# Quantised FFN at the end of a two-layer kernel: GpSimd scales the second half of the hidden blocks, and VectorE's and ScalarE's order changes

## The chip, the cores and the metric

The kernel runs on one core of a Trainium2 chip. Five engines work side by side, each through its own queue in order: TensorE (PE; its weight loads are shown as PEld), VectorE (DVE), ScalarE (ACT), GpSimd (POOL), and SyncE (SP), which here issues transfers. They meet through semaphores. The metric is the device time of one execution in microseconds; shown is a median of three runs. The profile is of one other execution.

## The reference, cut to what matters

Two layers on x of 16 x 256 tokens by 256 features. Only the last step, the quantised FFN of layer 1, is touched:

```python
def fake_quant_nvfp4(x, global_scale):          # blocks of 16 elements
    amax = jnp.max(jnp.abs(xb), axis=-1, keepdims=True)
    sc8 = clip(amax / 6 * global_scale, 0, 448).astype(float8_e4m3fn)
    dq = sc8 / global_scale
    a = jnp.clip(jnp.abs(xb) / safe_dq, 0.0, 6)
    q = jnp.sign(xb) * _FP4_VALS[jnp.digitize(a, _FP4_MIDS)]
    return (q * dq).reshape(sh)

gate_out = nvfp4_linear(x, gate_w, s_in)        # 256 -> 1024, x and w both quantised
up_out = nvfp4_linear(x, up_w, s_in)
hidden = silu(gate_out) * up_out
out = x + nvfp4_linear(hidden, down_w, s_in_down)   # 1024 -> 256, hidden quantised
```

## The kernel before

The 4096 tokens are 32 tiles of 128. The stage takes them in eight groups of four tiles. Each group is quantised as two pairs: `hh[0]` holds the hidden values of tiles 0 and 1 (128 partitions x 2048 f32), `hh[1]` those of tiles 2 and 3. There is no planner: every engine's program is written out by hand, six of the eight groups run in a loop, and semaphores count what is done.

VectorE's `group(g)` is a software pipeline. It quantises the hidden values of group g while it makes those of group g+1 (tiles t to t+3, with t = 4g + 4):

- `hidden_sizes` and `rows_sizes` (line 1837 and 1839): maxima over blocks of 16, from absolute values that ScalarE wrote (`s_ah`, `s_ax`).
- `block_scales` (1843 to 1849): the e4m3 scales and, in `inv4`, their reciprocals.
- `rows_scaled` (1871): the next rows x4 times their reciprocals. ScalarE then writes them as f16 (`rows_half`, 773), VectorE clamps (1877), rounds (1880) and multiplies by the scale (1886, `xq`).
- `hidden_scaled(p)` (1874): pair p of `hh` times the reciprocals of its blocks, into `wraw[:, p]`. ScalarE writes the f16 `hf[p]` from it (`hidden_half`, 972), VectorE clamps (1877), rounds (1880) and multiplies by the scale (`hidden_quantised`, 2169, `hq[p]`).
- `product(t, u)` (2177): silu times up, in two halves of 512 columns, from a bank and from `sil`, into `hh[u // 2]`.
- `results(g-1)` (2184): the down product of the group before, from banks 1 and 7, plus the residual X2, into `yo`, in two steps k = 0 and 1.

ScalarE's `group(i)` runs in this order: `rows_half`, the copies of turned hidden values for the down product (`hidden_out`, 985), `hidden_half(i, 0)`, the copy of the turned rows (`x_out`, 954), `hidden_half(i, 1)`, then `silu` (962) of four tiles in turn with `hidden_size` (absolute values, 967), and the norm of later rows (765, 769).

TensorE's loop turns quantised rows (1432) and hidden values (1462), multiplies down (1473), and then `ahead` runs gate (1441) and up (1450) of the four tiles; a gate product waits for the silu of the tile before, an up product for the product on VectorE. GpSimd does nothing in this stage, and SyncE sends `yo` out.

Of the kernel before, what the change touches and what calls it, by code (L numbers as in the profile page):

```python
# [7 lines left out]
ALU = mybir.AluOpType  # L8
# [9 lines left out]
P = 128  # L18
EPS = 1e-5
FAR = 1.0e6  # L20
FP4_MAX, FP8_MAX, BLOCK = 6.0, 448.0, 16
# [39 lines left out]
def two_layers_kernel(nc, x, itok, ctxT, ctxO, mask, w_redT, wgT, W1, b1, W2, b2,  # L61
# [8 lines left out]
    NTILE = NT // P  # L70
# [34 lines left out]
    with es:  # L105
# [3 lines left out]
        def sem(name):  # L109
            return es.enter_context(nc.semaphore(name))  # L110
# [71 lines left out]
        inv = sb("inv", [P, NIX], F32, ea)  # L182
# [88 lines left out]
        hh = [sb(f"hh{h}", [P, NQ], F32, ec) for h in range(2)]  # L271
# [8 lines left out]
        wraw = sb("wraw", [P, 3, FT * D], F32, ec)  # L280
# [38 lines left out]
        NBX, NBH = 4 * D // BLOCK, 2 * NQ // BLOCK  # L319
# [4 lines left out]
        inv4, scb = carve(5120, 320, F32), carve(5440, 160, BF16)  # L324
# [3 lines left out]
        def top(a):  # L328
# [23 lines left out]
        s_idle = sem("s_idle")  # L352
# [5 lines left out]
        s_S, s_sub, s_exp, s_pT, s_pTe, s_pv, s_cn, s_cT, s_cTe, s_wo, s_fin = [  # L358
            sem(n) for n in ("s_S", "s_sub", "s_exp", "s_pT", "s_pTe", "s_pv", "s_cn", "s_cT", "s_cTe", "s_wo", "s_fin")]
# [4 lines left out]
        n_cb, n_xn, n_ct, n_xt, n_kv, n_kb, n_q, n_qe = [sem(n) for n in ("n_cb", "n_xn", "n_ct", "n_xt", "n_kv", "n_kb", "n_q", "n_qe")]  # L364
        n_kc, n_va, n_bo = s_cke, s_cve, s_wo
        n_S, n_add, n_fo, n_sub, n_exp, n_pT, n_pTe, n_pv = [sem(n) for n in ("n_S", "n_add", "n_fo", "n_sub", "n_exp", "n_pT", "n_pTe", "n_pv")]
        n_cn, n_cT, n_cTe, n_wo, n_fin = [sem(n) for n in ("n_cn", "n_cT", "n_cTe", "n_wo", "n_fin")]
        s_wl, s_wmx, s_war, s_wq, s_wT, s_wTe = [sem(n) for n in ("s_wl", "s_wmx", "s_war", "s_wq", "s_wT", "s_wTe")]
        s_dst, s_dsd, s_xq, s_xqT, s_xqe, s_gm, s_um, s_sil, s_hq, s_hT, s_hTe, s_dn, s_y = [
            sem(n) for n in ("s_dst", "s_dsd", "s_xq", "s_xqT", "s_xqe", "s_gm", "s_um", "s_sil", "s_hq", "s_hT", "s_hTe",  # L370
                             "s_dn", "s_y")]
        s_h, s_gs, s_nm2, s_x4 = sem("s_h"), sem("s_gs"), sem("s_nm2"), sem("s_x4")
        s_ax, s_ah, s_vx, s_vh, s_fx, s_fh = [sem(n) for n in ("s_ax", "s_ah", "s_vx", "s_vh", "s_fx", "s_fh")]
        s_out = sem2("s_out")
# [90 lines left out]
        def _(pool):  # L465
# [166 lines left out]
            with pool.Else():  # L632
# [7 lines left out]
                for k in range(1, SLOTS):  # L640
                    weight_scaled(k)


        @block.scalar
        def _(act):
# [310 lines left out]
            def silu(t, u, first=False):  # L956

                for k in range(2):
                    act.wait_ge(s_gm, 2 * t + (k + 1))
                    if not first:  # L960
                        act.wait_ge(s_h, 2 * t + (k - 3))
                    act.activation(sil[:, u % 2, k * 512:(k + 1) * 512], bank[2 + k][:], ACT.Silu,  # L962
                                   scale=gmx[:, 8:9]).then_inc(s_sil, 1)

            def hidden_size(t, u):
                act.wait_ge(s_h, 2 * t + 2)
                act.activation(absh[:, u * FF:(u + 1) * FF], top(hh[u // 2][:, (u % 2) * FF:(u % 2 + 1) * FF]),
                               ACT.Abs).then_inc(s_ah, 1)

            def hidden_half(g, p):  # L970
                act.wait_ge(s_vh, g * 2 + (p + 1))
                act.mul(hf[p][:], top(wraw[:, p, :]), ABOVE).then_inc(s_fh, 1)

            x_out(0)
# [12 lines left out]
            def group(i, first=False, last=False):  # L987
                t = i * 4 + 4
                rows_half(i + 1)
                if not first:  # L990
                    hidden_out(i - 1, 2)
                hidden_half(i, 0)
                if not first:
                    hidden_out(i - 1, 3)
                x_out(i + 1)
                hidden_half(i, 1)
                silu(t, 0)
                silu(t + 1, 1)
                hidden_size(t, 0)
                silu(t + 2, 2)  # L1000
                hidden_size(t + 1, 1)
                silu(t + 3, 3)
                hidden_size(t + 2, 2)
                hidden_size(t + 3, 3)
                if not last:
                    tile_norm(i + 2)
                hidden_out(i, 0)
                hidden_out(i, 1)
# [499 lines left out]
        def _(v):  # L1508
# [364 lines left out]
            def hidden_scaled(p):  # L1873
                tt(blocks(wraw[:, p, :], 2), blocks(hh[p][:], 2), each_block(inv4[:, pair_c[p]], 2), ALU.mult).then_inc(s_vh, 1)
# [110 lines left out]
            with v.If(narrow == 1):  # L1985
# [89 lines left out]
                b = NB - 1  # L2075
# [92 lines left out]
            def hidden_quantised(p):  # L2168
                tt(blocks(hq[p][:], 2), blocks(hf[p][:], 2), each_block(scb[:, pair_c[p]], 2), ALU.mult).then_inc(s_hq, 1)

            def product(t, u):

                for k in range(2):
                    v.wait_ge(s_sil, 2 * t + (k + 1))
                    v.wait_ge(s_um, 2 * t + (k + 1))
                    o = (u % 2) * FF + k * 512
                    v.scalar_tensor_tensor(hh[u // 2][:, o:o + 512], bank[4 + k][:], gmx[:, 11:12],  # L2177
                                           sil[:, u % 2, k * 512:(k + 1) * 512], ALU.mult, ALU.mult).then_inc(s_h, 1)

            def results(g, ks=(0, 1)):  # L2180
                for k in ks:
                    v.wait_ge(s_dn, g * 4 + (2 * k + 2))
                    v.wait_ge(s_out[k], g * 16 + 16)
                    v.scalar_tensor_tensor(yo[:, k], bank[(1, 7)[k]][:].rearrange("p (t d) -> p t d", t=2), gmx[:, 10:11],
                                           X2[:, bass.ds(g * 4 + (2 * k + 1), 2), 0:D], ALU.mult, ALU.add).then_inc(s_y, 2)

            def group(g, later):

                t = g * 4 + 4
                hidden_sizes(g, st)  # L2190
                rows_sizes(g + 1, st)
                block_scales(slice(0, NBX + NBH), st)
                rows_scaled()
                hidden_scaled(0)
                rows_quantised(g + 1, st)
                hidden_scaled(1)
                v.wait_ge(s_fh, g * 2 + 1)
                clamped(hf[0][:], st)
                rounded(hf[0][:], st)
                if later:  # L2200
                    v.wait_ge(s_hT, g * 4)
                hidden_quantised(0)
                product(t, 0)
                v.wait_ge(s_fh, g * 2 + 2)
                clamped(hf[1][:], st)
                if later:
                    results(g - 1, (0,))
                product(t + 1, 1)
                rounded(hf[1][:], st)
                product(t + 2, 2)  # L2210
                hidden_quantised(1)
                product(t + 3, 3)
                if later:
                    results(g - 1, (1,))

            for u in range(4):
                product(u, u)
# [5 lines left out]
            g = NTILE // 4 - 1  # L2223
            hidden_sizes(g, st)
            block_scales(hid_c, st)
            for p in range(2):
                hidden_scaled(p)
            results(g - 1)
            for p in range(2):
                v.wait_ge(s_fh, g * 2 + (p + 1))  # L2230
# [74 lines left out]
```

## Time and profile before

| | |
|---|---|
| median of 3 runs | 811.55 us (811.29 to 814.38) |
| the profiled execution: time, span | 814.53 us, 812.8 us |
| busy, whole span: PE, PEld | 632.9, 461.9 us |
| busy, whole span: DVE, ACT, POOL | 623.2, 413.8, 211.3 us |
| first maximum of hidden sizes, groups 0 to 7 (start, us) | 587.01, 614.72, 643.22, 671.36, 699.66, 728.17, 755.97, 784.22 |
| copies of turned rows in the six loop groups (start, us) | 629.55, 657.68, 685.99, 714.50, 742.27, 770.55 |
| first recorded gate matmul in the same groups (start, us) | 631.22, 659.08, 687.39, 716.36, 744.05, 771.95 |

Times are from the span's start. The busy sums are averages over stages with different limits: GpSimd's 211.3 us all lie before the FFN stage. The three lower lines are taken from the instructions in order of time; they mark the same three points of each group, so differences between them show how regular the groups are. In a row of the trace an arrow reads "out<-in", and what stands in brackets is how long the engine was idle before the instruction, and who ended that. In a row of busy time by stretch stand the stretch, its length, the busy us (and instructions) of PE, PEld, DVE, ACT and POOL, the granted TensorE clock (PEclk, 1 is full speed), the DMA share and GB/s.

### The profile page before, as it was taken

The page shows a single profiled execution, that of the slowest core. Times are in us where ns is not written, and L with a number is a line of the kernel's source. Part 1 is how long each engine was busy: PE and PEld are TensorE (multiplying, and loading weights), DVE is VectorE, ACT ScalarE, POOL GpSimd, SP SyncE. Part 2 cuts the span into 40 slices and gives each one's busy share as a digit, 9 for nine tenths or more (in the row PEclk, how much of TensorE's full clock was granted, in tenths as well). Part 3 has the DMA queues.
Part 4 walks back from the last instruction along what each step waited for, and adds up shares of the span by engine and source line. Part 5 has one row for each costly group of instructions (what it writes and reads, how often), then busy time and mean ns, then how long its engine had stood idle before and what let it go on. Part 6 is the DMA issues. An engine that isn't in the chain of part 4 may idle for free.

```text
span 812.8 us, 14049 instructions
## 1 busy us (share of the span) xinstructions
PE 632.9 (78%) x3935; PEld 461.9 (57%) x3944; DVE 623.2 (77%) x1541; ACT 413.8 (51%) x698; POOL 211.3 (26%) x259
## 2 busy tenths in 40 slices
PE   6499982599999997687989999996545675567564
PEld 3387661377666775476888888876113333234333
DVE  5288888866566654677888998887599899989994
ACT  1333331233233332354556766657757777687664
POOL 6537755245554454101112132011000000000000
PEclk9699996699999999688999999999656887787797
DMA  8885553622122200600000000000000000000001
GB/s 323 266 310 200 202 178 111 189 86 72 48 61 61 71 27 24 209 0 2 0 0 0 0 0 0 0 2 1 4 0 1 26 13 13 26 26 13 13 26 52
DMA packets 30957, 53.99 MB, mean 66 GB/s; under 512 B 4973, under 2 KB 23806, under 8 KB 29760
## 3 DMA queue, kind: packets, MB, share of 16 engines
q1 hardware_dynamic: 24768, 39.29, 14.7%
q0 software_dynamic: 5568, 13.61, 4.8%
q10 hardware_dynamic: 576, 0.55, 0.2%
q8 instruction: 20, 0.33, 0.2%
q14 instruction: 25, 0.20, 0.1%
HBM read 39.38 MB, written 15.93 MB: 68 GB/s over the span
## 4 chain that ended last, share of the span: by engine, by line
DVE 22%; PE 21%; issue 8%; ACT 7%; DVEq 1%; POOL 0%; ACTq 0%; DMA 0%; POOLq 0%
PE bank L1276 4%; PE quad L1260 3%; DVE hh L2177 3%; PE bank L1291 2%; PE bank L1473 2%; DVE ctxs L1849 2%; DVE nS L1997 2%; DVE nM L2002 2%; DVE ctxs L1837 2%; DVE nS L2005 2%; ACT x L765 2%; PE quad L1251 1%; PE quad L1450 1%; PE quad L1441 1%; PE bank L1234 1%
## 5 line engine op out<-in xcount | busy, mean ns | idle before, releaser
L1473 PE MATMUL bank<-dT,hqT 128*128 128x256 bf16 x256 | 53.6, 380 | 44.3 <-ACT hqT L985 44.1
L1139 PE MATMUL quad<-W1s,xts 128*128 x160 | 75.6, 613 | 0.1
L1156 PE MATMUL bank<-W2s,hidT 128*128 x320 | 72.5, 379 | 0.3 <-ACT hidT L717 0.3
L1156 PEld LDWEIGHTS bank<-W2s,hidT 128*128 128x128 f32 x320 | 60.0, 190 | 12.6 <-issue 5.3
L606 POOL TENSOR_TENSOR X<-fo,X 128x256 f32<-128x256 f32 (+1 forms) x32 | 21.9, 683 | 169.1 <-DVE fo L2019 155.2
L1473 PEld LDWEIGHTS bank<-dT,hqT 128*128 128x128 bf16 x256 | 32.4, 134 | 56.4 <-ACT hqT L985 46.5
L713 ACT ACTIVATE hid<-hid 128x512 f32<-128x512 f32 x40 | 25.3, 633 | 76.7 <-DVE hid L1757 76.7
L1276 PE MATMUL bank<-nVB,nPT 128*128 128x34 f32 x512 | 63.0, 279 | 0.0
L1276 PEld LDWEIGHTS bank<-nVB,nPT 128*128 128x128 f32 x512 | 59.6, 191 | 3.7
L546 POOL DMA_INDIRECT x_after_ffn<-row,niU x40 | 39.4, 984 | 71.1 <-DVE row L1769 52.9
L2177 DVE SCALAR_TENSOR_TENSOR hh<-quad,gmx,sil 128x512 f32<-128x512 f32 x64 | 45.1, 745 | 11.5 <-PE quad L1450 8.5
L1757 DVE TENSOR_TENSOR hid<-quad,b1s 128x512 f32<-128x512 f32 x40 | 27.7, 692 | 32.4 <-PE quad L1139 32.4
L819 ACT COPY nPT<-quad 128x1024 f32<-128x1024 f32 x32 | 32.5, 1015 | 36.0 <-PE quad L1260 35.8
L1139 PEld LDWEIGHTS quad<-W1s,xts 128*128 128x128 f32 x160 | 29.8, 195 | 33.2 <-issue 32.1
L1260 PE MATMUL quad<-ident,nS 128*128 128x128 f32 x256 | 37.1, 292 | 13.0 <-DVE nS L1997 11.8
L512 POOL DMA_INDIRECT rows_by_expert<-row,pi x38 | 38.1, 1004 | 28.5 <-DVE pi L1660 19.0
L1088 PE MATMUL quad<-ctxs,hid 128*128 x160 | 41.3, 412 | 4.7 <-ACT hid L663 2.1
L505 POOL DMA_INDIRECT xg<-in_x,idxu x38 | 37.2, 978 | 26.8 <-DVE lgt L1616 11.2
L962 ACT ACTIVATE sil<-quad,gmx 128x512 f32<-128x512 f32 x64 | 40.5, 683 | 3.9 <-PE quad L1441 2.1
L1450 PE MATMUL quad<-uT,xqT 128*128 128x512 bf16 x128 | 37.2, 399 | 6.7 <-DVE hh L2177 5.4
L2005 DVE TENSOR_TENSOR nS<-nS,nM 128x512 f32<-128x512 f32 x64 | 41.4, 688 | 1.1
L1997 DVE TENSOR_TENSOR nS<-quad,maskS 128x1024 f32<-128x1024 f32 x32 | 39.0, 1219 | 3.9 <-PE quad L1251 3.9
(324 smaller groups left out, 1519.5 us busy)
## 6 DMA issues: line engine op xcount, KB each, us to landing
row<-rows_by_expert SPq DMA_DIRECT2D x40, 134.0 KB, 2.1
W1s<-in_ctxO SPq DMA_DIRECT2D x4, 1024.0 KB, 8.0
ctxs<-in_ctxT SPq DMA_DIRECT2D x4, 1024.0 KB, 14.6
W1s<-in_W SPq DMA_DIRECT2D x8, 512.0 KB, 3.9
W2s<-in_W SPq DMA_DIRECT2D x8, 512.0 KB, 5.4
out<-yo SPq DMA_DIRECT2D x16, 256.0 KB, 2.1
X<-x_after_ffn SPq DMA_DIRECT2D x7, 516.0 KB, 6.8
b1s<-in_b SPq DMA_DIRECT2D x1, 2048.0 KB, 8.3
```

The lines of the kernel that those rows point to most:

```text
L546: pool.indirect_dma_start(x2_d, bass.IndirectOffsetOnAxis(ap=niU[:, h, u:u + 1], axis=0), row[h][:, u, 0:XW], None, bounds_check=NT - 1, o ...
L962: act.activation(sil[:, u % 2, k * 512:(k + 1) * 512], bank[2 + k][:], ACT.Silu, scale=gmx[:, 8:9]).then_inc(s_sil, 1)
L1088: ins = pe.matmul(quad[:, u, 0:CW], xz[g % 2][:, u, z, c, :], ctxs[:, bass.ds(ex, 1), c, :].rearrange("p o s -> p (o s)"), start=z + c == ...
L1139: ins = pe.matmul(bank[2 + u % 2][:], xt[:, u, c, :], W1s[:, bass.ds(ex, 1), c, :].rearrange("p o s -> p (o s)"), start=c == 0, stop=c == ...
L1156: ins = pe.matmul(bank[6 + u % 2][:, 0:D], hidT[:, u % 2, c, :], W2s[:, bass.ds(ex, 1), c, :].rearrange("p o s -> p (o s)"), start=c == 0, ...
L1260: ins = pe.transpose(turned[:, k, c * P:(c + 1) * P], nS[q][:, 4 * k + 2 * c:4 * k + 2 * c + 2, :].rearrange("p h s -> p (h s)"), ident[:])
L1276: ins = pe.matmul(bank[7][:, n * 2 * VW:(n + 1) * 2 * VW], nPT[q][:, k, c * P:(c + 1) * P], nVB[h][:, n, :], start=True, stop=True)
L1450: ins = pe.matmul(bank[4 + k][:], xqT[:, u, c, :], uT[:, c, k * 512:(k + 1) * 512], start=c == 0, stop=c == DC - 1)
L1473: ins = pe.matmul(bank[(1, 7)[u // 2]][:, (u % 2) * D:(u % 2 + 1) * D], hqT[:, u % 2, c, :], dT[:, c, :], start=c == 0, stop=c == FT - 1)
L1997: tt(nS[q][:].rearrange("p (k m) s -> p k m s", k=4), scored.rearrange("p k (m s) -> p k m s", m=4), maskS[:, q, S - KW:S].unsqueeze(1).un ...
L2005: tt(half, half, bc(nM[q][:, HG * k:HG * k + HG], KW), ALU.subtract).then_inc(n_sub, 1)
L2177: v.scalar_tensor_tensor(hh[u // 2][:, o:o + 512], bank[4 + k][:], gmx[:, 11:12], sil[:, u % 2, k * 512:(k + 1) * 512], ALU.mult, ALU.mult ...
```

## The change

`hidden_scaled(1)` goes from VectorE to GpSimd, for all eight groups, as one multiply of 128x2048 f32 that signals `s_vp`. GpSimd starts it when VectorE has quantised the first pair (`s_hq`), in the last group when the scales are done (`s_iv`). VectorE does both steps of `results` and the products of tiles t and t+1 in that time, then waits for `s_vp`, since product t+2 overwrites `hh[1]`. The clamp and rounding of `hf[1]` move behind product t+2. ScalarE's `hidden_half(i, 1)` moves behind `hidden_size(t + 1)`. Three semaphores get one name with three of the other branch of the attention. The diff, without the lines that make the semaphores:

```diff
@@ gpsimd
+            for g in range(NTILE // 4):
+                if g < NTILE // 4 - 1:
+                    pool.wait_ge(s_hq, 2 * g + 1)
+                else:
+                    pool.wait_ge(s_iv, 1)
+                if g:
+                    pool.wait_ge(s_fh, 2 * g)
+                pool.sem_inc(s_idle, 1)
+                inv = inv4[:, NBX + NBH // 2:NBX + NBH].rearrange("p (t b) -> p t b", t=2)
+                pool.tensor_tensor(wraw[:, 1, :].rearrange("p (t k b) -> p t k b", t=2, k=BLOCK),
+                                   hh[1][:].rearrange("p (t k b) -> p t k b", t=2, k=BLOCK),
+                                   inv.unsqueeze(2).broadcast_to([P, 2, BLOCK, inv.shape[2]]), ALU.mult).then_inc(s_vp, 1)
@@ scalar
-                act.wait_ge(s_vh, g * 2 + (p + 1))
+                act.wait_ge((s_vh, s_vp)[p], g + 1)
...
-                hidden_half(i, 1)
                 silu(t, 0)
                 silu(t + 1, 1)
                 hidden_size(t, 0)
                 silu(t + 2, 2)
                 hidden_size(t + 1, 1)
+                hidden_half(i, 1)
                 silu(t + 3, 3)
@@ vector, group(g, later)
                 rows_quantised(g + 1, st)
-                hidden_scaled(1)
                 v.wait_ge(s_fh, g * 2 + 1)
...
                 hidden_quantised(0)
+                if later:
+                    results(g - 1)
                 product(t, 0)
+                product(t + 1, 1)
+                v.wait_ge(s_vp, g + 1)
+                product(t + 2, 2)
                 v.wait_ge(s_fh, g * 2 + 2)
                 clamped(hf[1][:], st)
-                if later:
-                    results(g - 1, (0,))
-                product(t + 1, 1)
                 rounded(hf[1][:], st)
-                product(t + 2, 2)
+                product(t + 3, 3)
                 hidden_quantised(1)
-                product(t + 3, 3)
-                if later:
-                    results(g - 1, (1,))
@@ vector, last group
-            for p in range(2):
-                hidden_scaled(p)
+            v.sem_inc(s_iv, 1)
+            hidden_scaled(0)
             results(g - 1)
```

VectorE's queue in the loop, before, from the quantising of the first pair (`hq`, line 2169) on; `hh` rows are products, `qb` rows are the clamp (1877) and rounding (1880) of the second pair, `yo` rows the results:

```order
L2169 TENSOR_TENSOR hq<-qb,ctxs 128x2048 [waits s_hT,s_v]
...
L2177 SCALAR_TENSOR_TENSOR hh<-quad,gmx,sil 128x512 [waits s_um,s_sil]
...
L1877 TENSOR_SCALAR qb<-qb 128x2048 [waits s_fh]
...
L2184 SCALAR_TENSOR_TENSOR yo<-bank,gmx,X 128x512
...
L1880 TENSOR_SCALAR qb<-qb 128x2048
...
L2169 TENSOR_TENSOR hq<-qb,ctxs 128x2048
...
L2184 ISA [waits s_out1,s_dn]
```

The same stretch of the changed kernel, whose lines are 14 further on (2169 is 2183, 1877 is 1891, 1880 is 1894, 2177 is 2191, 2184 is 2198):

```order
L2183 TENSOR_TENSOR hq<-qb,ctxs 128x2048 [waits s_hT,s_v]
...
L2198 SCALAR_TENSOR_TENSOR yo<-bank,gmx,X 128x512
...
L2191 SCALAR_TENSOR_TENSOR hh<-quad,gmx,sil 128x512 [waits s_um,s_sil]
...
L2188 ISA [waits s_vp]
...
L1891 TENSOR_SCALAR qb<-qb 128x2048 [waits s_fh]
L54 REGISTER_ALU
L1894 TENSOR_SCALAR qb<-qb 128x2048 [waits s_v]
...
L2183 TENSOR_TENSOR hq<-qb,ctxs 128x2048
```

Both results stand ahead of the products now; clamp and rounding of the second pair stand together between the third product and the last, and the second quantising ends the group.

ScalarE's queue in the last group before the end, which is written out without the loop's register instructions, before (`xqT` is the copy of the turned rows, `qb` the second hidden half, `sil` the silus, `ctxs<-hh` the absolute values):

```order
L954 COPY xqT<-bank 128x1024 [waits s_xqT]
L972 ACTIVATE qb<-wraw 128x2048 [waits s_vh]
L962 ACTIVATE sil<-quad,gmx 128x512 [waits s_h,s_gm] x4
L967 ACTIVATE ctxs<-hh 128x1024 [waits s_h]
L962 ACTIVATE sil<-quad,gmx 128x512 [waits s_h,s_gm] x2
```

and in the changed kernel:

```order
L968 COPY xqT<-bank 128x1024 [waits s_xqT]
L976 ACTIVATE sil<-quad,gmx 128x512 [waits s_h,s_gm] x4
L981 ACTIVATE ctxs<-hh 128x1024 [waits s_h]
L976 ACTIVATE sil<-quad,gmx 128x512 [waits s_h,s_gm] x2
L981 ACTIVATE ctxs<-hh 128x1024 [waits s_h]
L986 ACTIVATE qb<-wraw 128x2048 [waits s_vp]
L976 ACTIVATE sil<-quad,gmx 128x512 [waits s_h,s_gm] x2
```

The second half stood between the copy and the first silu; it stands behind the absolute values of the second tile, and waits for GpSimd.

## Rows read from the trace of the kernel before

**Rows 1.** Busy time by stretch, two loop groups: length, then the engines in turn.

```profile
643.22:671.36 28.14, 17.65 (x103) 9.89 (x104) 25.94 (x37) 21.28 (x26) 0.00 (x0) 0.82 0.05 19
699.66:728.17 28.51, 18.44 (x103) 10.69 (x104) 25.94 (x37) 21.27 (x26) 0.00 (x0) 0.76 0.05 18
```

**Rows 2.** Order of time, VectorE, one loop group: start, length, instruction, idle before.

```profile
699.66 2.41 DVE L1837 TENSOR_TENSOR ctxs<-ctxs 128x2048 bf16<-128x2048 bf16 x3 [0.46 <-ACT ctxs L967]
...
716.04 1.23 DVE L2169 TENSOR_TENSOR hq<-qb,ctxs 128x2048 bf16<-128x2048 f16 x1
717.93 1.41 DVE L2177 SCALAR_TENSOR_TENSOR hh<-quad,gmx,sil 128x512 f32<-128x512 f32 x2 [0.67 <-ACT sil L962]
...
722.29 0.68 DVE L1880 TENSOR_SCALAR qb<-qb 128x2048 int16<-128x2048 int16 x1
723.19 1.41 DVE L2177 SCALAR_TENSOR_TENSOR hh<-quad,gmx,sil 128x512 f32<-128x512 f32 x2 [0.22 <-PE quad L1450]
...
725.64 1.40 DVE L2177 SCALAR_TENSOR_TENSOR hh<-quad,gmx,sil 128x512 f32<-128x512 f32 x2
...
728.17 2.41 DVE L1837 TENSOR_TENSOR ctxs<-ctxs 128x2048 bf16<-128x2048 bf16 x3 [0.46 <-ACT ctxs L967]
```

**Rows 3.** Order of time, ScalarE, the same group.

```profile
710.98 1.91 ACT L972 ACTIVATE qb<-wraw 128x2048 f16<-128x2048 bf16 x1 [0.24 <-DVE wraw L1874]
...
714.50 1.01 ACT L954 COPY xqT<-bank 128x1024 bf16<-128x1024 bf16 x1 [0.71 <-PE bank L1432]
715.41 1.91 ACT L972 ACTIVATE qb<-wraw 128x2048 f16<-128x2048 bf16 x1
717.22 1.26 ACT L962 ACTIVATE sil<-quad,gmx 128x512 f32<-128x512 f32 x2
718.68 1.27 ACT L962 ACTIVATE sil<-quad,gmx 128x512 f32<-128x512 f32 x2 [0.20 <-DVE hh L2177]
719.84 1.05 ACT L967 ACTIVATE ctxs<-hh 128x1024 bf16<-128x1024 bf16 x1
720.78 1.26 ACT L962 ACTIVATE sil<-quad,gmx 128x512 f32<-128x512 f32 x2
```

**Rows 4.** Order of time, TensorE, the same group.

```profile
714.25 1.92 PE L1473 MATMUL bank<-dT,hqT 128*128 128x256 bf16 x8
716.36 0.81 PE L1441 MATMUL quad<-gT,xqT 128*128 128x512 bf16 x3 [0.18 <-issue]
...
717.95 1.18 PE L1441 MATMUL quad<-gT,xqT 128*128 128x512 bf16 x4
```

**Rows 5.** Order of time, ScalarE, TensorE, VectorE: first group, then that of 643.22.

```profile
607.07 0.69 ACT L962 ACTIVATE sil<-quad,gmx 128x512 f32<-128x512 f32 x1 [0.17 <-PE quad L1441]
...
609.74 1.06 ACT L967 ACTIVATE ctxs<-hh 128x1024 bf16<-128x1024 bf16 x1
...
614.72 2.41 DVE L1837 TENSOR_TENSOR ctxs<-ctxs 128x2048 bf16<-128x2048 bf16 x3 [1.12 <-ACT ctxs L967]
...
657.68 1.01 ACT L954 COPY xqT<-bank 128x1024 bf16<-128x1024 bf16 x1 [0.33 <-PE bank L1432]
...
659.08 0.81 PE L1441 MATMUL quad<-gT,xqT 128*128 128x512 bf16 x3 [0.19 <-issue]
```

**Rows 6.** Groups by line: GpSimd's multiplies; one VectorE line (ns min/median/max, first and last start).

```profile
L540 POOL TENSOR_TENSOR row<-xts,row 128x1024 f32<-128x1024 f32 x10 | 23.5, 2351 | 1.8 <-POOL xts L535 1.8
...
L580 POOL TENSOR_TENSOR wt<-wraw,wblk 128x512 f32 x6 | 6.4, 1060 | 0.0
L580 POOL TENSOR_TENSOR wt<-wraw,wblk 128x256 f32 x6 | 4.4, 727 | 0.0
...
L1764 DVE SCALAR_TENSOR_TENSOR row<-bank,sco,row x40: 483/484/485, 164.5 to 320.6; 128x256 f32<-128x256 f32 x40
```

**Rows 7.** Order of time, VectorE, the last group.

```profile
790.03 4.49 DVE L1874 TENSOR_TENSOR wraw<-hh,ctxs 128x2048 f32<-128x2048 f32 x2
...
800.46 0.69 DVE L1877 TENSOR_SCALAR qb<-qb 128x2048 f16<-128x2048 f16 x1
```

More of the change, by code:

```diff
@@ L366, in two_layers_kernel @@
         n_S, n_add, n_fo, n_sub, n_exp, n_pT, n_pTe, n_pv = [sem(n) for n in ("n_S", "n_add", "n_fo", "n_sub", "n_exp", "n_pT", "n_pTe", "n_pv")]
-        n_cn, n_cT, n_cTe, n_wo, n_fin = [sem(n) for n in ("n_cn", "n_cT", "n_cTe", "n_wo", "n_fin")]
+        n_cn, n_cT, n_cTe = s_cn, s_cT, s_cTe
+        n_wo, n_fin = [sem(n) for n in ("n_wo", "n_fin")]
         s_wl, s_wmx, s_war, s_wq, s_wT, s_wTe = [sem(n) for n in ("s_wl", "s_wmx", "s_war", "s_wq", "s_wT", "s_wTe")]
@@ L371, in two_layers_kernel @@
                              "s_dn", "s_y")]
+        s_iv, s_vp = sem("s_iv"), sem("s_vp")
         s_h, s_gs, s_nm2, s_x4 = sem("s_h"), sem("s_gs"), sem("s_nm2"), sem("s_x4")
```

## The prediction

> **What bounds the kernel now.** I read the page's table of slices for the stretch of the quantised FFN (from about 575 us to the end), then the busy time by stretch, then VectorE's, ScalarE's and TensorE's instructions in order of time for one group, and last the two ends of the stage. The change lies in that stage alone. It is eight groups of four token tiles; six of them run in a loop. I cut at the first maximum of the hidden sizes (L1837, 128x2048). A loop group of 28.51 us has VectorE busy for 25.94 us, ScalarE for 21.27 and GpSimd for nothing [rows 1]; so VectorE looks like the bound, and a copy of 2.28 us taken from it looks like a gain of nearly that. The rows in order of time say otherwise. All offsets below are from the group's start at 699.66.
>
> VectorE ends the quantising of hq0 at 17.61 (16.38 + 1.23), but its first product starts at 18.27, after 0.67 us idle that ScalarE's silu ends [rows 2]. That silu starts at 17.56, the very moment ScalarE is through with the second hidden half (L972, 15.75 to 17.66), which follows the copy of the turned rows at X = 14.84 (L954) back to back [rows 3]. So already now the group hangs on ScalarE's order as much as on VectorE's busy time: group length is X + 13.67 (28.51 - 14.84); the same subtraction gives 13.67 to 13.70 in all six loop groups, whose lengths are 27.80 to 28.51, mean 28.25, and whose X are 14.10 to 14.84. TensorE starts the gate matmuls at G = 16.70 (first one recorded; one of four has no record), after the copy and after its last down product (14.59 to 16.51) [rows 3, 4]. G - X is 1.86 here and 1.40 in the group of 657.68 (659.08 - 657.68) [rows 5]; over the six it is 1.40 three times, and 1.67, 1.78, 1.86.
>
> **What is removed.** One hidden_scaled on VectorE for each of eight groups: two take 4.49 us in a row, so one is 2.28 long and gives 2.20 back [rows 7]. In a loop group this does not move the clamp of hf0 by 2.20: the clamp waits for ScalarE's first half, which ends at 13.23 (11.32 + 1.91) [rows 3]. The clamp moves from 14.93 to 13.27; hq0 ends about 16.0 instead of 17.61. Gain up to here 1.6 us.
>
> **What GpSimd is given.** A 128x2048 f32 multiply of two SBUF operands, started when hq0 is done, about 16.1. No row has this size. Bounds: four times the 128x512 one is 4.2 us, the slope between 512 and 256 columns gives 3.1, twice the 128x1024 one is 4.7, and eight times the 256-column one 5.8 [rows 6]. I take 4.7, from the nearest size: done at 20.8. It is needed at two places: VectorE's third product, not before about G + 5.05 = 21.8 for other reasons (below), and ScalarE's second half at G + 6.4 = 23.1, or 22.3 where G is at its lowest, 15.86 (659.08 - 643.22) [rows 1, 5]. So up to 6.1 us of GpSimd time costs nothing. Beside it VectorE runs two results and four half products, all with one operand in a bank. The nearest rows are the 40 L1764 (bank and SBUF), part of which lie beside GpSimd's L535 and L540: 483 to 485 ns, all alike [rows 6]; I cost contention at nothing. The Trainium skill (SBUF — State Buffer, Who interferes with whom) says the same more widely: a VectorE instruction with at most one SBUF input outside the two-port modes leaves GpSimd alone, one with two SBUF inputs blocks it or is blocked. The Trainium skill (GPSIMD Engine Reference, Performance versus the Vector engine) gives 4497 ns for a 2048-column f32 add; by it the operation ends at 20.6 and the sum is the same.
>
> **What is moved, and costs.** ScalarE's second half (1.91 us) goes from before the first silu to behind hidden_size(t+1), that is, into the middle of the chain of silus, and VectorE's clamp of hf1 waits for it with product(t+3), hq1 and the next group behind it in its queue. I walk it from G:
> - silu(t) no longer waits for the half; it starts 0.72 behind its first gate matmul, as silu(t+1) does behind its own (717.95 to 718.68) [rows 3, 4]. Three gate matmuls of 0.38 take 0.81 together, so they follow at 0.215; the first of four stands at G - 0.21 by that, and after four gate and four up matmuls the gates of t+1 can start at G + 1.50, where now it is G + 1.59 (717.95) [rows 4]. TensorE, not ScalarE, sets this: the early silu gains 0.10 us only. silu(t+1) starts at G + 2.22.
> - From there ScalarE has no hole: silu pair 1.16 (718.68 to 719.84), hidden_size 0.94 (to 720.78), the same two again, half 1.91: 6.11 [rows 3]. What these wait for is in time: product(t) ends at G + 2.8, product(t+1) at G + 4.5, before hidden_size(t+1) at G + 5.47. The half ends at G + 8.33.
> - VectorE, done with product(t+2) at G + 6.5, stands idle until G + 8.37: a new wait of 1.9 us. Then clamp 0.72 (of the rounding's size), rounding 0.90 to the next product (722.29 to 723.19), and 2.53 from the last product's start to the next group (725.64 to 728.17; now results k=1 fills it, afterwards hq1; both fit below the last hidden_size) [rows 2]. The group is over at G + 12.52.
>
> So a group changes by (G + 12.52) - (X + 13.67) = (G - X) - 1.15: by 0.25 where G - X is 1.40, by 0.71 where it is 1.86. The six sum to 9.51 - 6.90 = +2.6 us. X itself rests on the sizes, the scaling of the rows, ScalarE's first half and the rows' transposes, none of which moves.
>
> The first group stands outside the loop, and there TensorE is late with the gates of the second tile (silu at 607.07 waits for it) [rows 5]. So nothing comes earlier: hidden_size(t+1) is at 609.74 as before, the half runs 610.68 to 612.59, the clamp starts at 612.63, the last product at 614.25, and 2.53 later, at 616.8, comes the next group, now 614.72 [rows 5]: +2.0 us.
>
> The last group: VectorE's hidden_scaled(1) goes (2.2 us), but results k=1 waits for the down product behind ScalarE's first half, as now. GpSimd starts when the scales are done, beside hidden_scaled(0), which has two SBUF inputs (790.03). Even if it must wait for that one (792.3), it is done at 797.0 and the half at 798.9; hf1 is clamped at about 800.46 [rows 7]. Cost 0. The renamed semaphores cost nothing: their uses lie in two branches of which one runs.
>
> **Sum.** +2.6 + 2.0 + 0 = +4.6 us on the profiled execution, whose span is 812.8 and whose time 814.5. That one was slower than the median, 811.55; I put the difference on the median: 816.2.
>
> **Rivals.**
> 1. TensorE at the higher clock. G and X follow the granted clock: mean 0.76 in the group of 699.66 and 0.82 in that of 643.22 [rows 1]. If each group had the best X seen (14.10) and G - X of 1.40, it would last 28.02, against 28.25 now: -1.4, with the first group +0.6, so 812.2: not slower. For it: silus and gates come in one denser piece. Against: TensorE's pause ahead of the next group's down products grows by the same amount, which speaks for the lower clock (0.71 in every group gives +6.3, 817.9, and X of 14.84 everywhere 1.6 more, 819.5). It decides from G = 15.4 on (28.25 - 12.52, less a sixth of the 2.0).
> 2. VectorE's busy time is the bound after all, and ScalarE's half somehow fits: 2.20 us times seven is -15.4, so 796.2. Against it stands the unbroken row of ScalarE instructions.
> 3. GpSimd is slower than 6.1 us, from its access pattern or from a neighbour: each us more delays the half in seven groups; at 7.0 us +6.3 on top, 822.5.
> 4. In the last group GpSimd gets the port first and VectorE's hidden_scaled(0) waits out its 4.7 us: first half, down product and both results follow, 820.9. The rows show no such meeting. The Trainium skill (SBUF — State Buffer, Who interferes with whom) has it that whichever starts first keeps the port for its whole instruction. VectorE needs no semaphore there and GpSimd does, so VectorE should be first.
>
> **Chances.** Forecast 0.56, rival 1 0.22, rival 2 0.06, rival 3 0.08, rival 4 0.08. The likeliest case has its own range of 814 to 819.5 (every group at +0.25, and X at its highest). The range reaches down into rival 1 and up into rival 4: 811.8 to 821.3. A change below 0.5% (4.1 us) can't be told from none. Of the forecast's chance some 0.21 falls below 815.6, with rival 1 0.42 for no change; 0.35 + 0.16 = 0.51 slower; 0.07 faster.
>
> **What would show it.** In the profile after: loop groups of about 28.7 us with VectorE busy 23.7; some 1.9 us idle before the clamp of hf1, ended by ScalarE's half; silu(t) 1.0 us earlier at most and silu(t+1) 0.1; GpSimd 4.2 to 4.8 us, done before the third product; first interval 29.7 instead of 27.71; last group unchanged. Groups of 26 us would prove the walk wrong, and a wait on GpSimd or results longer than 0.75 us beside it would prove the free cover wrong.

## The result, and the profile after

The changed kernel takes 817.81 us (median of 5 runs, 814.13 to 821.25); the kernel before takes 812.05 (5 runs, 811.29 to 814.38). The ratio is 1.0071, with a 95% interval of 1.0044 to 1.0098: slower by 5.8 us, little, but outside what the measurement blurs.

The first page line of the changed kernel shows that the work was moved as meant. VectorE was busy for 623.2 us before and is for 13.6 us less now, GpSimd for 38.1 us more than 211.3:

```profile
PE 625.1 (77%) x3935; PEld 463.0 (57%) x3944; DVE 609.6 (75%) x1533; ACT 413.5 (51%) x698; POOL 249.4 (31%) x267
```

The engine that looked fullest got lighter, and the kernel got slower. Busy time by stretch, three loop groups after (columns as in [rows 1]):

```profile
642.49:671.66 29.17, 17.76 (x103) 10.89 (x104) 24.19 (x37) 21.16 (x26) 4.54 (x1) 0.68 0.05 18
700.41:729.64 29.23, 17.76 (x103) 10.86 (x104) 24.19 (x37) 21.16 (x26) 4.54 (x1) 0.68 0.05 18
729.64:758.35 28.71, 16.72 (x103) 10.25 (x104) 24.10 (x37) 21.15 (x26) 4.54 (x1) 0.80 0.05 18
```

Against [rows 1], VectorE's 25.94 us have become 24.1 to 24.2 (23.7 had been expected), GpSimd's nothing 4.54, and the length of the six loop groups has gone from 27.80 to 28.51 up to 28.68 to 29.23. The granted TensorE clock is lower, too: 0.68 in every other group, where no loop group before was under 0.76.

VectorE in the group of 700.41, in order of time; the rows answer to [rows 2]:

```profile
700.41 2.41 DVE L1851 TENSOR_TENSOR ctxs<-ctxs 128x2048 bf16<-128x2048 bf16 x3
...
713.68 0.69 DVE L1891 TENSOR_SCALAR qb<-qb 128x2048 f16<-128x2048 f16 x1 [0.45 <-ACT qb L986]
...
715.14 1.23 DVE L2183 TENSOR_TENSOR hq<-qb,ctxs 128x2048 bf16<-128x2048 f16 x1
716.28 1.57 DVE L2198 SCALAR_TENSOR_TENSOR yo<-bank,gmx,X 128x512 f32<-128x512 f32 x2
718.46 1.41 DVE L2191 SCALAR_TENSOR_TENSOR hh<-quad,gmx,sil 128x512 f32<-128x512 f32 x2 [0.61 <-PE quad L1464]
720.18 1.41 DVE L2191 SCALAR_TENSOR_TENSOR hh<-quad,gmx,sil 128x512 f32<-128x512 f32 x2 [0.32 <-PE quad L1464]
722.15 1.41 DVE L2191 SCALAR_TENSOR_TENSOR hh<-quad,gmx,sil 128x512 f32<-128x512 f32 x2 [0.56 <-ACT sil L976]
725.47 0.69 DVE L1891 TENSOR_SCALAR qb<-qb 128x2048 f16<-128x2048 f16 x1 [1.91 <-ACT qb L986]
...
727.11 1.41 DVE L2191 SCALAR_TENSOR_TENSOR hh<-quad,gmx,sil 128x512 f32<-128x512 f32 x2 [0.21 <-DVE qb L1894]
...
729.64 2.41 DVE L1851 TENSOR_TENSOR ctxs<-ctxs 128x2048 bf16<-128x2048 bf16 x3
```

The first pair is quantised at 15.96 us into the group (before: 17.61). That lead of 1.65 us melts in waits of 0.61, 0.32 and 0.56 us at the products, for TensorE and ScalarE (the first result too has moved ahead of them); then VectorE stands 1.91 us before the clamp of the second pair, released by ScalarE's half. ScalarE, the same group, answering to [rows 3]:

```profile
715.26 1.01 ACT L968 COPY xqT<-bank 128x1024 bf16<-128x1024 bf16 x1 [0.71 <-PE bank L1446]
717.60 1.27 ACT L976 ACTIVATE sil<-quad,gmx 128x512 f32<-128x512 f32 x2 [1.33 <-PE quad L1455]
719.33 1.27 ACT L976 ACTIVATE sil<-quad,gmx 128x512 f32<-128x512 f32 x2 [0.46 <-PE quad L1455]
720.49 1.05 ACT L981 ACTIVATE ctxs<-hh 128x1024 bf16<-128x1024 bf16 x1
721.43 1.27 ACT L976 ACTIVATE sil<-quad,gmx 128x512 f32<-128x512 f32 x2
722.57 1.07 ACT L981 ACTIVATE ctxs<-hh 128x1024 bf16<-128x1024 bf16 x1
723.52 1.92 ACT L986 ACTIVATE qb<-wraw 128x2048 f16<-128x2048 bf16 x1
```

From 719.33 to 725.44 there is no hole. Where the half stood before, right behind the copy, ScalarE now waits 1.33 us for the gates (0.88 where the clock is higher). It gave up a slot that cost nearly nothing for one in the middle of the chain. GpSimd's part, in that group and in the last:

```profile
716.57 4.54 POOL L654 TENSOR_TENSOR wraw<-hh,ctxs 128x2048 f32<-128x2048 f32 x1 [24.22 <-DVE hq L2183]
...
793.57 6.56 POOL L654 TENSOR_TENSOR wraw<-hh,ctxs 128x2048 f32<-128x2048 f32 x1 [14.52 <-DVEq L2238]
```

In seven groups it takes 4.52 to 4.56 us; in the last, beside VectorE's `hidden_scaled(0)`, 6.56. TensorE in the group of 700.41: the first down product behind its pause of 8.49 us, the last one ahead of the gates, and the first recorded gate matmul (G = 16.70):

```profile
704.39 1.89 PE L1487 MATMUL bank<-dT,hqT 128*128 128x256 bf16 x8 [8.49 <-ACT hqT L999]
...
715.02 1.91 PE L1487 MATMUL bank<-dT,hqT 128*128 128x256 bf16 x8
717.11 0.81 PE L1455 MATMUL quad<-gT,xqT 128*128 128x512 bf16 x3 [0.18 <-issue]
```

### The profile page after: what moved, and what is told of

The parts are those of the page before. It is cut to its first block, busy times and chain, and to the rows that moved or that the text cites. A ratio compares the mean times of both kernels' runs of the same rounds, so it can differ in the third digit from the quotient of the medians.

```text
span 816.1 us, 14059 instructions
## 1 busy us (share of the span) xinstructions
PE 625.1 (77%) x3935; PEld 463.0 (57%) x3944; DVE 609.6 (75%) x1533; ACT 413.5 (51%) x698; POOL 249.4 (31%) x267
## 4 chain that ended last, share of the span: by engine, by line
PE 24%; DVE 19%; ACT 8%; issue 7%; DVEq 1%; POOL 0%; ACTq 0%; DMA 0%; POOLq 0%
PE bank L1290 4%; PE quad L1455 3%; PE quad L1274 3%; PE bank L1487 2%; PE bank L1305 2%; DVE ctxs L1863 2%; PE quad L1464 2%; DVE nS L2011 2%; DVE nM L2016 2%; ACT qb L986 2%; DVE ctxs L1851 2%; DVE nS L2019 2%; ACT x L779 2%; PE quad L1265 1%; DVE x L1885 1%
## 5 line engine op out<-in xcount | busy, mean ns | idle before, releaser
L654 POOL TENSOR_TENSOR wraw<-hh,ctxs 128x2048 f32<-128x2048 f32 x8 | 38.4, 4795 | 196.1 <-DVE hq L2183 181.5
```

The costliest lines, as they stand in the source:

```text
L654: pool.tensor_tensor(wraw[:, 1, :].rearrange("p (t k b) -> p t k b", t=2, k=BLOCK), hh[1][:].rearrange("p (t k b) -> p t k b", t=2, k=BLOC ...
```

## The experiments

Single executions of one kernel differ by up to 1.2% (805.14 to 814.58 us for the kernel before on one chip). In the traces most of that lies ahead of this stage: its first maximum of hidden sizes starts anywhere from 579.9 to 587.2 us, while the stage itself takes 231.1 to 231.9 us in the changed kernel, e5, e6 and e7. So the table gives, beside the ratio of run times (each against runs of the kernel before on its own chip), what the trace shows of the stage: from that first maximum (before: 587.01, span 812.8) to the end, the mean of the six loop groups, and the last group.

| kernel | median us | ratio to before (95%) | stage | loop group | last group |
|---|---|---|---|---|---|
| before | 812.05 | 1 | 225.8 | 28.25 | 28.58 |
| changed | 817.81 | 1.0071 (1.0044 to 1.0098) | 231.9 | 28.96 | 28.56 |
| e1_mul_vector | 823.18 | 1.0159 (1.0106 to 1.0212) | 236.1 | 29.65 | 28.61 |
| e2_gps_f16 | 803.39 | 0.9919 (0.9887 to 0.9950) | 219.7 | 27.24 | 28.36 |
| e3b_both_f16 | 804.58 | 0.9896 (0.9863 to 0.9928) | 217.4 | 27.08 | 27.57 |
| e4_before_f16 | 809.86 | 0.9969 (0.9939 to 1.0000) | 222.4 | 27.97 | 26.62 |
| e5_tail | 818.20, one run | none | 231.6 | 28.96 | 28.55 |
| e6_half_mid | 818.40 | 1.0103 (1.0049 to 1.0157) | 231.1 | 28.96 | 28.51 |
| e7_gps_plus1 | 818.33 | 1.0081 (1.0051 to 1.0110) | 231.9 | 28.96 | 28.56 |
| e8_gps_plus4 | 829.40 | 1.0230 (1.0174 to 1.0285) | 242.4 | 30.52 | 29.16 |
| e9_fill_short | 814.16 | 1.0010 (0.9979 to 1.0041) | 226.5 | 27.99 | 28.97 |
| e10_fill_both | 819.80 | 1.0085 (1.0056 to 1.0115) | 231.5 | 28.09 | 33.36 |
| e12_last_on_vector | 803.95 | 0.9894 (0.9856 to 0.9932) | 217.7 | 27.24 | 26.27 |

**The multiply back on VectorE.**

```diff
                 rows_quantised(g + 1, st)
+                hidden_scaled(1)
                 v.wait_ge(s_fh, g * 2 + 1)
...
-                v.wait_ge(s_vp, g + 1)
                 product(t + 2, 2)
```

> The changed kernel with the multiply of the second pair put back on VectorE (right behind the rows' quantising), all orders of the change kept. Theory (ScalarE's order sets the group): VectorE's 2.2 us hardly matter. The second half stays behind hidden_size(t+1); only hidden_size(t) comes about 0.5 us later, since results and product(t) end later. Loop groups about 29.4 us against 28.96 in the changed kernel, VectorE's idle before the clamp of hf1 about 0.9 instead of 1.9; whole kernel 3 us over the changed one. Rival 1 (GpSimd's multiply, as a neighbour or as something waited for, makes the group long): without it the groups fall to 28.3 or less, and the kernel to 812. Rival 2 (VectorE's busy time is the bound): groups grow by the full 2.2, to 31.2, and the kernel by 15 us.

Measured: loop groups of 29.65 us, 0.7 over the changed kernel, and a stage 4.2 us longer; VectorE does 26.13 us in the group of 703.57. Its clamp still waits for ScalarE's half:

```profile
729.07 0.70 DVE L1879 TENSOR_SCALAR qb<-qb 128x2048 f16<-128x2048 f16 x1 [1.78 <-ACT qb L974]
```

Both rivals fall. Without GpSimd the groups don't return to 28.3, so GpSimd is not what makes them long; and taking 2.2 us off VectorE is worth 0.7 us in this order, so VectorE's busy time isn't either. This run also splits the change in two: the new orders alone make a group 1.40 us longer (29.65 against 28.25), and GpSimd's multiply gives 0.70 of that back. I had expected the wait to fall to 0.9; it is 1.78, because the third product came later too, by about as much as the half.

**ScalarE's second half dropped.** GpSimd's output is f16 and goes straight into `hf[1]`; so it waits for the quantising of the pair before (`s_hq`) and no longer for a half.

```diff
-                pool.tensor_tensor(wraw[:, 1, :].rearrange("p (t k b) -> p t k b", t=2, k=BLOCK),
+                pool.tensor_tensor(hf[1][:].rearrange("p (t k b) -> p t k b", t=2, k=BLOCK),
...
                 hidden_size(t + 1, 1)
-                hidden_half(i, 1)
```

> The changed kernel, but GpSimd writes its product as f16 straight into hf[1], and ScalarE's second half (1.91 us) is dropped (the factor 1.003 and the cut to the upper 16 bits go with it, so rounding near the middle between two values differs). Theory: the half is what VectorE's clamp waits for; without it the clamp follows product(t+2) at once, loop groups about 27.0 us (28.96 - 1.9), first group about 27.5, last one unchanged, kernel about 803 to 805. Rival 1 (TensorE's lower clock makes the groups long): groups stay above 28. Rival 2 (GpSimd is what is waited for): the clamp then waits for GpSimd, and groups stay at 28 or more.

Measured: 27.24 us a group, 1.72 below the changed kernel, 803.39 us in all. In the group of 690.78 VectorE's clamp of the second pair follows the third product with no idle time:

```profile
712.56 1.41 DVE L2190 SCALAR_TENSOR_TENSOR hh<-quad,gmx,sil 128x512 f32<-128x512 f32 x2 [0.56 <-ACT sil L975]
713.89 0.68 DVE L1890 TENSOR_SCALAR qb<-qb 128x2048 f16<-128x2048 f16 x1
```

GpSimd's multiply in the same group is as long as with an f32 output:

```profile
706.90 4.54 POOL L653 TENSOR_TENSOR qb<-hh,ctxs 128x2048 f16<-128x2048 f32 x1 [22.68 <-DVE hq L2182]
```

This is the direct test of the theory: the 1.91 us wait before that clamp and the half go together. It also shows that a low clock alone doesn't make groups long: the granted clock here is 0.69.

**Both halves dropped.** VectorE's `hidden_scaled(0)` writes `hf[0]` as f16 as well. It ran twice; the first time gave 805.53 us, ratio 0.9924 (0.9893 to 0.9955), but no usable trace.

```diff
-                hidden_half(i, 0)
...
-                tt(blocks(wraw[:, p, :], 2), blocks(hh[p][:], 2), ...).then_inc(s_vh, 1)
+                tt(blocks(hf[p][:], 2), blocks(hh[p][:], 2), ...).then_inc(s_fh, 1)
```

> As the last, and VectorE writes hf[0] as f16 too, so ScalarE's halves are all dropped (the factor 1.003 and the cut to 16 bits with them). Theory: the first half only holds the clamp of hf0 by 0.45 us, which is given back at the products; loop groups stay within 0.3 us of the last kernel (27.0), but the last group loses about 3 us, since its first half stands ahead of the down product; kernel about 800. Rival (both halves are on the chain): groups lose another 1.9.

> The kernel in which GpSimd and VectorE write both hidden halves as f16 and ScalarE's halves are dropped (with the factor 1.003 and the cut to the upper 16 bits), again, for a trace of its groups. In its first timing it stood beside the kernel with only the second half dropped (805.5 and 803.4 us). Theory: the clamp of hf0 no longer waits (0.45 us), but the gates start when the turned rows are copied and after the last down product, as before, so the groups stay at 27.2; the last group is about 3 us shorter; kernel 799 to 802. Rival: dropping the first half lets the TensorE work ahead of the gates run earlier, at the lower granted clock, and nothing is gained: groups 27.2 to 27.6, and the 3 us of the last group are the only ones.

Measured: 27.08 us a group, near the 27.2 expected, but 804.58 us, not 799 to 802. (One of its six groups took 26.43, at a granted clock of 0.81; the others took 27.10 to 27.28, about as in e2 and e12.) The last group lost 1.0 us, not 3. The reason stands in that group's rows of VectorE:

```profile
782.86 2.29 DVE L1884 TENSOR_TENSOR qb<-hh,ctxs 128x2048 f16<-128x2048 f32 x1 [0.15 <-DVE ctxs L1859]
785.07 1.40 DVE L2194 SCALAR_TENSOR_TENSOR yo<-bank,gmx,X 128x512 f32<-128x512 f32 x2
786.39 3.67 DVE L1887 TENSOR_SCALAR qb<-qb 128x2048 f16<-128x2048 f16 x1
```

and of GpSimd:

```profile
782.97 6.54 POOL L653 TENSOR_TENSOR qb<-hh,ctxs 128x2048 f16<-128x2048 f32 x1 [13.13 <-DVEq L2233]
```

The clamp is 3.67 us long, in every other group 0.69. It ends at 790.06, 0.55 after GpSimd's multiply (789.51). The rows read as if each engine had held the other up once: GpSimd started 0.11 us behind the two-operand instruction and took 2.0 more than alone; the clamp, issued while GpSimd ran, took 3.0 more. The two results between them, with one operand in a bank, ran in 1.40. So the earlier start was taken back by a meeting that the faster tail itself had brought about. The Trainium skill (SBUF — State Buffer, Who interferes with whom) describes an exclusive lock held for a whole instruction, with tensor_scalar among the instructions that can take it; these rows agree in both directions.

**The last group's second pair on VectorE**, in the kernel with both halves dropped, to test that reading.

```diff
-            for g in range(NTILE // 4):
+            for g in range(NTILE // 4 - 1):
...
             for p in range(2):
+                if p:
+                    hidden_scaled(1)
                 v.wait_ge((s_fh, s_vp)[p], g + 1)
```

> The kernel with both halves written as f16 and no half on ScalarE, with the last group's second pair back on VectorE, behind the quantising of the first pair: scaled(0), results, clamp, rounding, hq0, scaled(1), clamp, rounding, hq1. In the trace of that kernel the first clamp of the last group took 3.67 us instead of 0.69 beside GpSimd's multiply. Theory (the two engines exclude each other there): every clamp is 0.69 again, hq0 ends 12.1 us into the last group instead of 15.1, the last group takes 25.3 us instead of 27.6; loop groups 27.1 as before; kernel 2 us less, about 802. Rival (the clamp waited for something else, the semaphore of the pair): a clamp of 3 us or more stays.

Measured:

```profile
783.85 1.40 DVE L2190 SCALAR_TENSOR_TENSOR yo<-bank,gmx,X 128x512 f32<-128x512 f32 x2
785.16 0.68 DVE L1883 TENSOR_SCALAR qb<-qb 128x2048 f16<-128x2048 f16 x1
```

Every clamp is short, and the first quantising ends 12.01 us into the last group, as worked out. That group takes 26.27 us, 1.3 less than 27.57 and not the 2.3 expected: the second quantising ends 16.92 us into the group, only 0.8 before e3b's 17.70, since VectorE now does the second multiply (2.28 us) between the two. The median is 803.95, ratio 0.9894; against e3b's 0.9896 the runs can't tell the two apart, and in the traces the stages are level, since e3b's first two groups were 1.5 us shorter (at clocks of 0.69 and 0.81, against 0.63 and 0.75) with the same instructions in both. e2, e3b and e12 beat the kernel before by about 1% and the changed one by 1.5 to 1.8%, but their rounding differs near the middle between two FP4 values.

**GpSimd's multiply in the last group released later.**

```diff
-            v.sem_inc(s_iv, 1)
             hidden_scaled(0)
+            v.wait_ge(s_vh, NTILE // 4)
+            v.sem_inc(s_iv, 1)
```

> The changed kernel, with GpSimd's multiply of the last group released only when VectorE's hidden_scaled(0) is done. In the changed kernel it started beside it and took 6.56 us instead of 4.54. Theory (it waited for VectorE's two-operand instruction): it takes 4.5 us again, is done at about the same time as now (12.7 us into the group), and the last group stays 28.5. Rival (the last group's operands or the wait on two semaphores made it long): it takes 6.5 us again and ends 2 us later.

Measured: 4.51 us instead of 6.56, and a last group of 28.55. The 2.0 us were waiting, and they were free here.

```profile
793.75 2.29 DVE L1888 TENSOR_TENSOR wraw<-hh,ctxs 128x2048 f32<-128x2048 f32 x1
...
796.30 4.51 POOL L654 TENSOR_TENSOR wraw<-hh,ctxs 128x2048 f32<-128x2048 f32 x1 [16.04 <-DVEq L2240]
```

**Both multiplies as f16 on VectorE, in the kernel before.** The same two lines as in e3b on the old orders, with nothing on GpSimd.

> The kernel before the change, with both multiplies on VectorE writing f16 and ScalarE's halves dropped (with the factor 1.003 and the cut to 16 bits); nothing on GpSimd. Theory: ScalarE's second half stood ahead of the first silu; without it the silu waits for the gates instead, 1.4 to 1.9 us after the copy of the turned rows instead of 2.7, but VectorE is nearly full (25.9 us busy), so only its idle of 0.3 to 0.7 us goes: loop groups 27.8 to 27.9, the last group 2 us shorter, kernel about 806. Against 27.2 with the multiply on GpSimd: so GpSimd's help is worth 0.6 us a group once ScalarE is out of the way. Rival (GpSimd's help is worth its full 2.2 us once ScalarE is out of the way): groups 28.2 or more here, or 26 there.

Measured: 27.97 us a group and 26.62 for the last; 809.86 us, a ratio of 0.9969 whose interval just reaches 1 (806 was expected). VectorE is busy for 25.88 us of a group of 27.78. Dropping the halves in their old places gives 0.28 us a group; dropping the second alone in its new place gave 1.72 (e2). That is the plainest measure of what the move cost. GpSimd's multiply together with the new orders, with ScalarE out of the way, is worth 0.7 to 0.9 us a group: 27.97 here against 27.24 (e12) and 27.08 (e3b), a third to two fifths of the 2.2 us it takes off VectorE. No run gives GpSimd's share without the orders.

**ScalarE's half elsewhere among the silus.**

```diff
                 hidden_size(t, 0)
+                hidden_half(i, 1)
                 silu(t + 2, 2)
                 hidden_size(t + 1, 1)
-                hidden_half(i, 1)
```

> The changed kernel with ScalarE's second half two places earlier, between hidden_size(t) and silu(t+2). Theory: the half is on the chain wherever it stands among the silus, since ScalarE has no hole there: loop groups 28.7 to 29.0, VectorE's wait moves from the clamp to product(t+2), GpSimd's multiply (4.55 us, done at 20.7) just in time; kernel within 2 us of the changed one. Rival (its place alone was the mistake): groups fall by 1 us or more, kernel to 811 or less.

Measured: 28.96 us, the same as in the changed kernel. In the group that ends at 724.51 the half itself waits 0.48 us for GpSimd (ScalarE's row):

```profile
716.51 1.91 ACT L986 ACTIVATE qb<-wraw 128x2048 f16<-128x2048 bf16 x1 [0.48 <-POOL wraw L654]
```

and VectorE's wait has moved to the third product and grown to 2.95:

```profile
719.03 1.41 DVE L2191 SCALAR_TENSOR_TENSOR hh<-quad,gmx,sil 128x512 f32<-128x512 f32 x2 [2.95 <-ACT sil L976]
```

So it isn't the one place that was ill chosen.

**More work for GpSimd ahead of its multiply.** One memset of 128x1032, and then two of 128x2048:

```diff
+                pool.memset(wraw[:, 2, 0:1032], 0.0)
                 pool.sem_inc(s_idle, 1)
```

> The changed kernel with a memset of 128x1032 f32 (0.96 us) into an unused buffer ahead of GpSimd's multiply in each group. Theory: the multiply is done 20.7 us into a group and first needed by product(t+2) at 21.7 and by ScalarE at 23.1, so nothing changes: groups 28.96 within 0.3, kernel 816 to 819. Rival (what waits for GpSimd makes the groups long): each group grows by 0.96, kernel by 7.

> The same with two memsets of 128x2048 (1.88 us each). Theory: the multiply is done at about 24.5 instead of 20.7, past both deadlines; ScalarE's half starts 1.4 us later than 23.1, and groups become 30.4 us, the kernel about 828. Rival (GpSimd has more room than thought, or a memset beside VectorE costs VectorE time of its own): no change, or more than 3.8 us a group.

Measured: 28.96 and 30.52 us. A delay of 0.92 us (719.43 to 720.35) costs nothing, one of 3.85 (690.67 to 694.52) costs 1.56; so GpSimd has 2.3 us to spare, as the rows of the changed kernel say (done at 20.70, ScalarE's half at 23.11). In e8 the multiply runs from 694.52 to 699.04, and both waits end with it, ScalarE's:

```profile
699.07 1.91 ACT L988 ACTIVATE qb<-wraw 128x2048 f16<-128x2048 bf16 x1 [1.67 <-POOL wraw L656]
```

and VectorE's:

```profile
699.38 1.41 DVE L2193 SCALAR_TENSOR_TENSOR hh<-quad,gmx,sil 128x512 f32<-128x512 f32 x2 [4.03 <-POOL wraw L656]
```

The last groups of the two runs show the meeting of VectorE and GpSimd again, in part. In e7 GpSimd's multiply starts when 1.41 us of `hidden_scaled(0)` are left, and takes 1.24 more than 4.54:

```profile
796.46 2.29 DVE L1889 TENSOR_TENSOR wraw<-hh,ctxs 128x2048 f32<-128x2048 f32 x1 [0.15 <-DVE ctxs L1864]
797.34 5.78 POOL L655 TENSOR_TENSOR wraw<-hh,ctxs 128x2048 f32<-128x2048 f32 x1
```

In e8 the multiply comes after `hidden_scaled(0)` and takes 4.50; the clamp is issued 0.47 us before its end (810.98) and takes 1.03 instead of 0.69. The two memsets beside `hidden_scaled(0)` kept their 3.67 us, and that kept its 2.29.

```profile
806.48 4.50 POOL L656 TENSOR_TENSOR wraw<-hh,ctxs 128x2048 f32<-128x2048 f32 x1 [0.18 <-POOL wraw L653]
810.51 1.03 DVE L1893 TENSOR_SCALAR qb<-qb 128x2048 f16<-128x2048 f16 x1
```

**TensorE kept busy in its pauses.** Extra matmuls into bank 7, whose content the next down product replaces:

```diff
                 down(i, 1)
+                for c in range(12):
+                    pe.matmul(bank[7][:, 0:D], identb[:], dT[:, c % FT, :], start=True, stop=True)
```

> The changed kernel with 12 extra matmuls (128x256 bf16, about 2.6 us at 1.2 GHz) into bank 7, which is overwritten afterwards, in TensorE's short pause of 2.8 us ahead of the second pair's last turned tile. It is to show why the copy of the turned rows stands at 14.81 us on average in the changed kernel and at 14.57 before. Theory (a lower granted clock, after longer pauses): with the short pause filled the last down product of the stage ahead of the gates takes 1.0 to 1.5 us in every group instead of 1.9 in every other one; gates start at 15.9 to 16.2 instead of 16.44 on average, groups 28.5, kernel 3 us below the changed one. Rival (the clock does not follow what TensorE does in that pause): groups go on alternating between 28.7 and 29.2.

> As the last, and 40 extra matmuls (4.3 us at 2.4 GHz) in the long pause of 8.5 us between the turned tiles and the first down product. Theory: the clock is at the higher level through the down products too; gates start at 15.8, groups 28.3 to 28.5, kernel 3 to 5 us below the changed one, which brings it to the level of the kernel before but not under it, since the second half still costs its 1.9 us. Rival: as before, no change; or more work lowers the clock later in the group, and groups get longer than 28.96.

Measured with the short pause filled: five groups of 28.00 us and one of 27.92, under the 28.25 of the kernel before, and 814.16 us in all, 1.0010 of it. TensorE in the group of 643.41, from the last turned tile to the gates:

```profile
655.07 1.04 PE L1487 MATMUL bank<-dT,hqT 128*128 128x256 bf16 x8
656.28 0.62 PE L1446 MATMUL bank<-identb,xq 128*128 128x128 bf16 x8 [0.17 <-DVE xq L1905]
657.60 1.05 PE L1487 MATMUL bank<-dT,hqT 128*128 128x256 bf16 x8 [0.70 <-ACT hqT L999]
658.85 0.81 PE L1455 MATMUL quad<-gT,xqT 128*128 128x512 bf16 x3 [0.20 <-issue]
```

The two down products ahead of the gates take 1.04 and 1.05 us (2.4 GHz), not 1.91 (1.2 GHz) as in the groups of 29.2, and the gates start at G = 15.44 instead of 16.70. The expected 28.5 was too careful: the copy of the turned rows comes earlier as well (14.03), which I had left out. Filling the long pause too brought nothing more (28.09, with one group of 28.59): the first down product behind the 40 matmuls still took 1.62 to 1.89 us in five of the six groups, so they did not do there what they were meant to. They also stand ahead of the last group's down products, where they cost 4.4 us (33.36 against 28.97): a miss of mine, since there that pause is no pause. No run puts the short filler into e2, whose four down products of each loop group took 1.89 to 1.92 us.

## Why the prediction was right

The direction, the mechanism and the place were right, and 816.2 lies 1.6 us under the measured median.

- **What is taken off VectorE does not shorten the group**: right. hq0 was expected at about 16.0 and ends at 15.96, and the lead is lost before the second clamp. Within the new orders the 2.2 us are worth 0.7 (e1), less than the 1.4 that the orders cost. VectorE busy for 23.7 us was too low; it is 24.1 to 24.2.
- **GpSimd's multiply**: 4.7 taken, 4.54 measured; done at 20.8 forecast, 20.70 measured. Contention at nothing: right, products beside it stay at 1.41 a pair, and results at 1.40 where the second doesn't await its down product (687.52, 745.50).
- **The walk from G**: silu(t+1) at G + 2.22, measured 719.33 - 717.11 = 2.22; the half's end at G + 8.33, measured 8.33; 1.9 us idle, measured 1.91; group length G + 12.52, measured 29.23 - 16.70 = 12.53, and 12.46 to 12.53 in all six groups.
- **"X itself rests on ... none of which moves"**: this term was mis-sized. X went from 14.57 to 14.81 on average and G from 16.16 to 16.44, so the loop groups grew by 0.70 each and not 0.43: +4.2 us, not +2.6. Most of it is X (0.24 of the 0.28). Ahead of X stand TensorE's last turned tile and a down product: before, the tile took 0.62 to 0.77 us in three groups of six (those with X of 14.10, 14.46 and 14.58); after, it took 0.97 to 1.03 in all six and the down product 1.91 or 1.92. In every other group the second down product took that long too. The granted clock went from 0.76 and 0.82 to 0.68 and 0.80. e9 shows that X and G do follow the clock and what TensorE does before: one filled pause moves them to 14.03 and 15.44.
- **Why the clock was lower** stays open. TensorE's pause ahead of the down products grew from 6.0 to 8.5 us, which I had named against rival 1 and carried into its other end only; but no run fills that pause alone, and its length does not decide by itself: e2 has 6.3 to 6.5 us and clocks of 0.69 to 0.75, e1 has 8.2 to 8.4 us and clocks of 0.72 to 0.80.
- **First group**: +2.0 forecast, 29.61 - 27.71 = +1.9 measured. **Last group**: 0 forecast, 28.56 against 28.58.
- **The narrow range**: its lower end of 814 does not follow from +0.25 us a group, which gives 811.55 + 1.5 + 2.0 = 815.1.
- The stage grew by 6.1 us (4.6 forecast). The profiled span grew by only 3.3 since that execution reached the stage 2.8 us earlier; the medians differ by 5.8.
- **Rival 1** needed a high clock, and the clock fell; but with the clock raised the same kernel is level with the one before (e9, 1.0010), as that rival's sum had it. **Rival 2** and **3** did not come; e8 shows 3 would, from 2.3 us more. **Rival 4**: VectorE was first, by 0.11 us, and GpSimd waited its 2.0 us at no cost.

## What to carry to other kernels

When an engine is over 90% busy and a group still ends at an instruction of another engine, walk the group in order before taking work from the full one: here 2.2 us off VectorE were worth 0.7 in the new orders, and a half of 1.9 us put into ScalarE's unbroken row cost 1.7, against 0.3 for both halves in their old places. Ask of an instruction that is moved what it stood beside: the old slot was next to a wait of 0.9 to 1.3 us, the new one next to none. And an instruction that can be folded into its producer (an output type, here) is worth more than one that is moved.

## What the hardware showed that I had not expected

- VectorE and GpSimd kept each other waiting both ways: a GpSimd multiply of 4.54 us took 6.56 behind VectorE's two-operand f32 instruction, and a VectorE f16 clamp of 0.69 us took 3.67 behind that multiply. With the overlap removed both were short again (e5, e12), and with less of it the excess was smaller (1.24 us in e7, 0.34 in e8). VectorE instructions with an operand in a bank kept their length. Such a wait shows in the trace as a long instruction, not as idle time.
- Twelve useless matmuls of about 1.5 to 2.2 us in TensorE's pause made the whole group 0.96 us shorter (28.96 to 28.00), by the clock at which the matmuls after them ran.
